# Solve steps on all four partition quarters, wider small products and clock products in a delta-rule transformer kernel

## What is computed

```
q, k = l2norm(silu(x @ Wq)), l2norm(silu(x @ Wk));  v = silu(x @ Wv);  beta = 2 sigmoid(x @ Wb)
S = 0                                    # per image slot and head, 32 x 32
for t in tokens:                         # the scan runs over the first axis
    S += beta_t * k_t (v_t - S^T k_t)^T
    o_t = S^T q_t
o = rmsnorm(o);  x += o @ Wo;  x += down(silu(gate(rmsnorm x)) * up(rmsnorm x))
```

## Time and profile before

| | us |
|---|---|
| median of 3 runs (lowest, highest) | 295.88 (294.21, 296.39) |
| the profiled execution's own time | 295.5 |
| its span | 293.7 |
| TensorE busy | 270.0 (92%) |
| VectorE busy | 202.3 (69%) |
| ScalarE busy | 92.4 (31%) |
| mean granted TensorE clock | 0.952 of full speed |

### The profile page before, as it was taken

The page is one execution under the profiler, slowest core; times in us unless marked ns, Lnnn a source line. Parts: engine busy times, 40 slices in busy tenths (PEclk is TensorE's granted clock), DMA queues, the critical chain, the costliest instruction groups (busy, mean ns, idle before and its releaser), DMA issues.

```text
span 293.7 us, 9894 instructions
## 1 busy us (share of the span) xinstructions
PE 270.0 (92%) x4473; PEld 207.1 (71%) x4473; DVE 202.3 (69%) x405; ACT 92.4 (31%) x231; POOL 37.9 (13%) x35
## 2 busy tenths in 40 slices
PE   8999999999999899978888999988889999789865
PEld 8666677778997788867756766867786676655443
DVE  3549869987689676367667579564646765498992
ACT  1122301330000036655215432654514343351210
POOL 1991100203893100000000000000000000000000
PEclk9999999999999999899968999977985999999999
DMA  7999900000000000000001203400000000000001
GB/s 288 417 423 420 436 25 0 0 0 2 0 0 2 0 1 3 2 2 2 2 4 43 104 1 111 192 4 2 1 4 2 0 2 0 0 1 2 0 0 45
DMA packets 2730, 18.71 MB, mean 64 GB/s; under 512 B 464, under 2 KB 784, under 8 KB 1936
## 3 DMA queue, kind: packets, MB, share of 16 engines
q1 hardware_dynamic: 2704, 18.34, 15.8%
HBM read 18.01 MB, written 0.33 MB: 62 GB/s over the span
## 4 chain that ended last, share of the span: by engine, by line
PE 77%; DVE 16%; ACT 3%; issue 3%; POOL 0%; DVEq 0%; POOLq 0%
PE ps L1258 12%; PE ps L1580 8%; PE ps L1302 5%; PE ps L1796 4%; PE ps L1316 4%; PE ps L1561 3%; PE ps L1681 3%; PE ps L1421 3%; PE ps L1690 3%; PE ps L1716 2%; DVE big L1110 2%; DVE wt L1107 2%; PE ps L1248 2%; PE ps L1838 2%; PE ps L1762 2%
## 5 line engine op out<-in xcount | busy, mean ns | idle before, releaser
L1258 PE MATMUL ps<-big,cwb 128*128 128x384 f32 x112 | 37.9, 489 | 0.0
L1258 PEld LDWEIGHTS ps<-big,cwb 128*128 128x128 f32 x112 | 21.0, 190 | 12.9
L1580 PE MATMUL ps<-xT,wl 128*128 128x320 f32 x88 | 24.5, 434 | 1.2 <-ACT wguT L369 1.2
L289 POOL TENSOR_TENSOR xs<-xs,big 128x640 f32<-128x640 f32 x14 | 23.3, 1665 | 1.4
L1580 PEld LDWEIGHTS ps<-xT,wl 128*128 128x128 f32 x88 | 16.6, 190 | 8.3 <-ACT wguT L369 1.6
L1681 PE MATMUL ps<-wt,big 32*32 32x32 f32 x1280 | 14.6, 198 | 4.7 <-DVE big L1110 2.3
L345 ACT COPY pecT<-ps 128x384 f32<-128x384 f32 x12 | 5.7, 478 | 41.5 <-PE ps L1258 41.5
L1681 PEld LDWEIGHTS ps<-wt,big 32*32 32x32 f32 x1280 | 13.0, 109 | 6.8 <-DVE big L1110 4.0
L1316 PE MATMUL ps<-wt,pecT 128*128 128x256 f32 x72 | 16.5, 381 | 0.6 <-DVE big L819 0.6
L1302 PE MATMUL ps<-wt,pecT 128*128 128x256 f32 x72 | 16.9, 381 | 0.0
L1107 DVE COPY_PREDICATED wt<-cst,ps 128x320 f32<-128x320 int32 x16 | 8.0, 499 | 12.1 <-PE ps L1690 12.1
(11 more groups left out here) (306 smaller groups left out, 534.5 us busy)
## 6 DMA issues: line engine op xcount, KB each, us to landing
big<-in_patches SPq DMA_DIRECT2D x6, 960.0 KB, 11.7
wl<-in_layers SPq DMA_DIRECT2D x2, 2176.0 KB, 19.7
wf<-in_ffn SPq DMA_DIRECT2D x1, 2112.0 KB, 17.8
wl<-in_layers SPq DMA_DIRECT2D x2, 1040.0 KB, 15.9
wt<-in_tok SPq DMA_DIRECT2D x1, 1536.0 KB, 24.7
wt<-in_tok SPq DMA_DIRECT2D x1, 768.0 KB, 8.5
cwb<-in_conv SPq DMA_DIRECT2D x1, 640.0 KB, 3.9
cst<-in_constants SPq DMA_DIRECT2D x1, 320.0 KB, 25.0
```

The costliest lines, as they stand in the source:

```text
L289: nc.gpsimd.tensor_tensor(xs[:, hf], old, new, ALU.add).then_inc(S["xsum"], 1)
L1258: last = mm(ps[:, i % 4, 0:GRP], cwc[:, k, c * P:(c + 1) * P], xg[:, g, k, :], start=(k == 0), stop=(k == KC - 1))
L1580: last = mm(ps[:, bank, 0:NT], w(c, j), x[:, c, :], start=(c == 0), stop=(c == CH - 1))
```

## The change

It makes these edits:
- `solve` runs over all four quarters both times. The product r gets a second one beside each, which multiplies a block of zeros (`nought`) into the even quarters, so that the sums there do not change when VectorE adds them.
- The semaphores of these copies are merged into `half_0` and `half_1`; the order of the waits is the same.
- Products of 1, 4 or 8 moving columns get `WIDE` = 64 columns; only those that were there before are read. `ug` moves into a dead part of `wt`, so that 64 columns can be read there.
- `keep_clock` products: one of 512 columns among each layer's value products, one of 256 behind the outputs, 512 in the place of 192 ahead of the global scores, one of 512 behind the first down product; the seven in the tail are split in two and five around a transposed weight block.
- ScalarE's `causal(8, 12)` stands ahead of the first `y_out` instead of behind it.

```diff
+WIDE = 64
...
+        nought = sb("nought", [P, 32])
...
-        ug = sb("ug", [P, CH, H])
...
-        heads = blk.rearrange("p (h d) -> p h d", h=HP)[:, :, 0]
+        heads = blk.rearrange("p (h d) -> p h d", h=HP)[:, :, 0:WIDE // HP]
...
+        ug = wt[:, T_GQ:T_GQ + 512].rearrange("p (c n) -> p c n", c=CH)
...
             nc.gpsimd.memset(ones[:, :], 1.0 / C).then_inc(S["ones"], 1)
+            nc.gpsimd.memset(nought[:, :], 0.0)
...
+                causal(8, 12)
                 y_out(1, 0)
                 act_.wait_ge(S["v_mm"], EACH["v_mm"] * l + 2)
                 nc.scalar.activation(vs[:, 0:8, :].rearrange("p g d -> p (g d)"), ps[:, 7, 0:C], ACT.Silu
                                      ).then_inc(S["silu"], 1)
-                causal(8, 12)
                 y_out(1, 1)
...
-                v.tensor_scalar(nsse, ps[:, 0, 0:NG], EPS_RMS, -1.0, ALU.add, ALU.mult).then_inc(S["ss"], 1)
+                sums = ps[:, 0, 0:PJ * WIDE].rearrange("p (g d) -> p g d", g=NG)[:, :, 0]
+                v.tensor_scalar(nsse, sums, EPS_RMS, -1.0, ALU.add, ALU.mult).then_inc(S["ss"], 1)
...
-                    last = mm(ps[:, 7, at:at + 1], sq[:, 0, t * P:(t + 1) * P], ones[:, 0:1], start=True, stop=True)
+                    last = mm(ps[:, 7, at:at + WIDE], sq[:, 0, t * P:(t + 1) * P], ones[:, 0:WIDE], start=True, stop=True)
...
             project(1)
-            keep_clock(0, 1, 192)
+            keep_clock(0, 1, 512)
...
-                            last = mm(ps[:, 5, H * p:H * p + H], hT[:, c, P * p:P * p + P], wb[:, c, :],
+                            at = L_B + H * c
+                            last = mm(ps[:, 5, H * p:H * p + WIDE], hT[:, c, P * p:P * p + P], wl[:, at:at + WIDE],
                                       start=(c == 0), stop=(c == CH - 1))
...
-                        mm(ps[:, 0, HP * pj:HP * pj + HP], kqsq[:, 0, pj % 2, P * p:P * p + P], heads, start=True, stop=True)
+                        mm(ps[:, 0, WIDE * pj:WIDE * (pj + 1)], kqsq[:, 0, pj % 2, P * p:P * p + P], heads, start=True,
+                           stop=True)
...
                 last.then_inc(S["v_mm"], 1)
+                keep_clock(5, 1, 512)
                 for c in range(CH):
                     last = mm(ps[:, 7, 0:C], hT[:, c, 0:P], wvb[:, c, :, 0:P], start=(c == 0), stop=(c == CH - 1))
...
-                def solve(rows, b):
+                def solve(b):
 
                     for g in range(NB * b, NB * (b + 1)):
-                        for q in rows:
+                        for q in range(4):
                             r = slice(32 * q, 32 * q + 32)
                             last = mm(ps[r, 4 + b, 32 * (g % NB):32 * (g % NB) + 32], ttc[r, g, :],
                                       bv[r, g, :], start=True, stop=True)
...
-                    solve((0, 2), b).then_inc(S["u1_mm"], 1)
+                    solve(b).then_inc(S["u1_mm"], 1)
...
                     for g in range(NB * b, NB * (b + 1)):
+                        cols = slice(32 * (g % NB), 32 * (g % NB) + 32)
                         for a in range(2):
-                            last = mm(ps[64 * a + 32:64 * a + 64, 6 + b, 32 * (g % NB):32 * (g % NB) + 32],
-                                      apm[64 * a:64 * a + 32, g, 32:64], uc[64 * a:64 * a + 32, g, :],
-                                      start=True, stop=True)
+                            early, late = slice(64 * a, 64 * a + 32), slice(64 * a + 32, 64 * a + 64)
+                            mm(ps[early, 6 + b, cols], nought[late, :], uc[late, g, :], start=True, stop=True)
+                            last = mm(ps[late, 6 + b, cols], apm[early, g, 32:64], uc[early, g, :], start=True, stop=True)
                     last.then_inc(S["r_mm"], 1)
...
-                    solve((1, 3), b).then_inc(S["u2_mm"], 1)
+                    solve(b).then_inc(S["u2_mm"], 1)
...
                 outputs(1).then_inc(S["o_mm"], 2)
+                keep_clock(5, 1, 256)
...
-                    last = mm(ps[0:n, p, 0:1], sqx[:, c, P * p:P * p + n], ones[:, 0:1], start=(c == 0), stop=(c == CH - 1))
+                    last = mm(ps[0:n, p, 0:WIDE], sqx[:, c, P * p:P * p + n], ones[:, 0:WIDE], start=(c == 0),
+                              stop=(c == CH - 1))
...
-            weights_across(6, 9)
-            keep_clock(5, 7)
+            weights_across(6, 8)
+            keep_clock(5, 2)
+            weights_across(8, 9)
+            keep_clock(5, 5)
...
                 last.then_inc(S["out_mm"], 1)
+                if p == 0:
+                    keep_clock(4, 1, 512)
```

More of the change, by code:

```diff
@@ L539, in layer @@
                 act_.wait_ge(S["u1_mm"], EACH["u1_mm"] * l + 1)
-                nc.scalar.copy(part_of(uc, 0), ps[:, 4, 0:NT]).then_inc(S["u1"], 1)
+                nc.scalar.copy(part_of(uc, 0), ps[:, 4, 0:NT]).then_inc(S["half_0"], 1)
                 act_.wait_ge(S["u2_mm"], EACH["u2_mm"] * l + 1)
-                nc.scalar.copy(part_of(uc, 0), ps[:, 4, 0:NT]).then_inc(S["u2"], 1)
+                nc.scalar.copy(part_of(uc, 0), ps[:, 4, 0:NT]).then_inc(S["half_0"], 1)
                 for j in range(CH):
@@ L879, in class_keys @@
                 dve.wait_ge(S["u"], 1)
-                v.tensor_tensor(ug[:, :, :], u[:, :, :],
+                v.tensor_tensor(ug[:, :, 0:H], u[:, :, :],
                                 vec[:, V_GKG:V_GKG + 2].unsqueeze(2).broadcast_to([P, CH, H]), ALU.mult
@@ L1129, in layer @@
                     v.tensor_tensor(part_of(bv, b), part_of(bv, b), ps[:, 6 + b, 0:NT], ALU.add
-                                    ).then_inc(S["b2"], 1)
+                                    ).then_inc(S["half_1"], 1)
                 dve.wait_ge(S["u2_mm"], EACH["u2_mm"] * l + 2)
-                v.tensor_copy(part_of(uc, 1), ps[:, 5, 0:NT]).then_inc(S["u2_two"], 1)
+                v.tensor_copy(part_of(uc, 1), ps[:, 5, 0:NT]).then_inc(S["half_1"], 1)
                 dve.wait_ge(S["lwb"], EACH["lwb"] * l + 16)
@@ L1360, in both_windows @@
                 for c in range(CH):
-                    mm(ps[:, b, at:at + n], stat[:, c, P * hf:P * hf + P], moving(c), start=(c == 0), stop=(c == CH - 1))
+                    mm(ps[:, b, at:at + WIDE], stat[:, c, P * hf:P * hf + P], moving(c, WIDE), start=(c == 0),
+                       stop=(c == CH - 1))
                 for a in range(2):
@@ L1364, in both_windows @@
                     for c in range(CH):
-                        last = mm(ps[64 * a:64 * a + 64, b, at + n:at + 2 * n], stat[:, c, cols], moving(c),
+                        last = mm(ps[64 * a:64 * a + 64, b, at + n:at + 2 * n], stat[:, c, cols], moving(c, n),
                                   start=(c == 0), stop=(c == CH - 1))
@@ L1633, in key_squares @@
                         p = pj // 2
-                        mm(ps[:, 0, HP * pj:HP * pj + HP], kqsq[:, 0, pj % 2, P * p:P * p + P], heads, start=True, stop=True)
+                        mm(ps[:, 0, WIDE * pj:WIDE * (pj + 1)], kqsq[:, 0, pj % 2, P * p:P * p + P], heads, start=True,
+                           stop=True)
                     for a in range(2):
-                        last = mm(ps[64 * a:64 * a + 64, 0, 4 * HP:5 * HP], kqsq[:, 0, a, NW:NT], heads, start=True, stop=True)
+                        last = mm(ps[64 * a:64 * a + 64, 0, 4 * WIDE:5 * WIDE], kqsq[:, 0, a, NW:NT], heads, start=True,
+                                  stop=True)
                     last.then_inc(S["ss_mm"], 1)
@@ L1753, in outputs @@
                     return last
-                pe.wait_ge(S["u2"], EACH["u2"] * l + 1)
-                pe.wait_ge(S["u2_two"], EACH["u2_two"] * l + 1)
+                pe.wait_ge(S["half_0"], EACH["half_0"] * (l + 1))
+                pe.wait_ge(S["half_1"], EACH["half_1"] * (l + 1))
                 outputs(0).then_inc(S["o_first"], 1)
```

15 lines of the change are left out of this document (9 added, 6 removed).

## The result

The changed kernel takes 311.15 us in the median of four runs (307.04 to 313.06), against 295.57 before, now in the median of four runs as well. By the ratio the change costs 13.0 us. The forecast was 306.8 us, 10.9 us or 3.7% slower, with a range up to 310.5. The interval holds 3.7%; the median over all four runs lies 0.65 us above the range. The profiled execution is the slowest of the four, 313.06 us, and has TensorE's clock at 0.934 on average where the fastest has 0.955; so its stretches are read one by one, and its span of 311.3 is not taken for the change's price.

What follows compares the result with a forecast made beforehand. It took TensorE's instruction supply, blocks 3.4 us apart in straight code of tiny matmuls, and half-clock stretches as bounds; 11.5 + 0.2 - 1.4 + 0.6 = +10.9 us on 295.5 gave 306.4, hence 306.8 us, range 299 to 310.5.

Steps and rivals of the forecast that it cites:

- The straight code's supply: Solve steps and product r: 240 more pairs a layer wait for instruction blocks 3.4 us apart; +11.5 us for both layers.
- The first rival: From u1 to the outputs, blocks come ahead of need and the clock holds 2.4 GHz: faster, 288.4 us; chance 0.13.
- the second: Solve steps: the next block's request leaves at once, only 2.35 us from request to use counts: 300.5 us; chance 0.13.
- the pace at the lower level is hidden by the waits: Solve steps: execution at 1.2 GHz adds nothing, as TensorE waits for instruction blocks anyway.
- block G: Layer 0's instruction block from 154.5, with 87 of u2, the query norm's two passes and 39 of the outputs.
- block H: Layer 0's instruction block from 157.9, with the last 41 output pairs, which end at 158.9; in layer 1, 37 pairs.
- Clock in the solve steps: 1.2 GHz from about u2 to the norm product behind the outputs, as before; no gain.
- Wide products ahead of the loop: Betas and key squares: +0.2 us for both layers; clock stays at 2.4 GHz through L1652, net 0.7 us earlier a layer.
- the term of -1.4 us: Both layers' net gain from 2.4 GHz in L1652 and the value products, less the added 512-wide product; bounds 0 and -2.2.
- The clock product behind the outputs: The 256-column product delays the norm product L1762 beyond TensorE's idle 0.59 us: 0.3 a layer, +0.6 us.
- nothing: Edits forecast to cost nothing, such as 64-wide statistics and window sums, tail clock products, causal scaling moved, renamed semaphores.
- The third rival: L1652 stays cold and waits hold the clock down behind the outputs: +1.4 and 1 to 2 more, about 310 us; chance 0.08.

Runs made afterwards that it cites:

- solve_only: The kernel before with only the solve steps and the product between them on four quarters: 308.3 us, ratio 1.042.
- the burst: The kernel before with 8 clock products and 512 tiny products (1024 matmuls) in straight code at the end of TensorE's program: 325.8 us; as a hardware loop 312.3.
- rest_only: The changed kernel with the solve steps and the product between them back on two quarters, all other edits kept: 297.4 us, ratio 1.005.

## Why the prediction was right, point by point

**The straight code's supply** was the step that decided, and it held: 24 blocks, three stops a layer at the predicted matmuls, the first block usable at 147.74 where 147.67 was forecast. The first rival (supply keeps up, 288.4 us) is refuted by `solve_only` and the burst, the second (blocks overlap their requests) by spacings that are never under 3.3 us.

**Its size was too small.** The term was +11.5 us, and the profiled execution shows +15.8 (7.7 and 8.0), `solve_only` +15.1 (7.9 and 7.2). The total came nearer, 13.0 us by the ratio against 10.9, because less than that reaches the whole time: in `solve_only` about 3 us came back elsewhere. No term stood for that, so it is in part luck that the range held the 308.6 us that the ratio gives. I took 3.4 us a block, from three spacings. Under full load it is 3.64 in the burst and 3.87, 3.74, 4.15 and 4.01 between resumptions in the changed kernel (147.74, 151.61, 155.35; 224.02, 228.17, 232.18). Both parts of a spacing were longer in the changed kernel: the next block was asked for 1.1 to 1.6 us after a resumption, not 1.0 to 1.1, and could be used 2.4 to 3.0 us after its transfer began, not 2.3 to 2.4. In layer 0 that puts block G at 155.35, not 154.5. And "the pace at the lower level is hidden by the waits" failed for the last piece: the rest of u2, the query norm and the outputs needed 4.7 us at half clock (155.35 to 160.07), so they ran until 160.1, and the wait for block H, which was to set the end at 158.9, did not matter. In layer 1 it did, with 0.43 us in the outputs at 236.20. From the first resumption to the end of the outputs it was 13.4 us there (224.02 to 237.41), where the forecast had 11.0; three spacings of 12.2 us instead of 10.2 are 2.0 of these 2.4.

**Clock in the solve steps**: no gain was forecast, and the stretch at 1.2 GHz grew from 6.8 and 10.3 to 13.7 us each: in layer 0 it now begins at about 147.5, in the first stop, where the forecast had it from u2 on. **Wide products ahead of the loop**: L1652 fell to 1.56 and 1.63 us; in layer 0 the first level product starts 0.72 us earlier (126.85 against 127.57), the net 0.7 that was worked out. The loop's end is only 0.3 us earlier in that layer, since a half-clock stretch fell into it (130.4 to 133.8, granted clock 0.51). As the profiles with narrow betas show, L1652 was not at half clock in all executions, so the term of -1.4 us was taken from one that had it in both layers. **The clock product behind the outputs** delays the norm product of layer 0: 0.83 us behind the start of the squares instead of 0.49, +0.34 against 0.3.

**What "nothing" hid.** Two clock products a layer were costed by their time alone. That they move every border behind them, and can put one into the loop's end for 1.8 us, was not in the sum. In the changed kernel they did not (its borders lie where I had counted them), in `rest_only` they did. The third rival's price, 1 to 2 us more behind the outputs, did not come: the way from layer 0's squares to layer 1's loop end is 1.0 us shorter. A range up to 312 would have been the honest one, with the spacing's upper end taken from the code under load and not from three single waits.

## What to carry to other kernels

Count instructions where matmuls are tiny: one that executes in 10 ns costs about 28 ns in straight code (3.64 us for 128 with their loads), and free lanes of the array are then not free. Where a wait shows "issue", look for a transfer of the instruction queue 2 to 3 us ahead of its end, and count matmuls between two such stops. In a hardware loop the same work is cheap (11.2 us for 1024 matmuls instead of 26.9), but see that no block begins in the loop's last instructions: its first pass stood still for 1.8 to 2.7 us there.

## What the runs showed that I had not expected

Sixteen matmuls of padding, 0.3 us of work, moved stops worth up to 2.7 us a layer. The clock of the same kernel differs between executions, 0.934 to 0.955 in the changed one, and with it the time by 6 us; a stretch at half clock in one profile is no property of the kernel until a second profile shows it. And what a solve stretch loses is not all lost to the kernel: 15.1 us in the two stretches of `solve_only` were 12.4 in its span.
